# A decoder layer on one core: keys in three slots, and a third PSUM bank for the logits

## The chip, the cores and the metric

The kernel runs on one core of a Trainium2 chip, in one launch. The metric is the device time of the launch in microseconds (us). Lower is better.

## The reference

One decoder layer on x of 16 sequences, 128 positions, 256 features, in float32. Three sublayers follow each other, each with a residual and a layer norm (post-norm). The change touches the second; cut to what matters:

```python
x = _layernorm(x + mixer(x))             # quantized linear layers, gated scan over the features
x = _layernorm(x + xattn(x, ctx, pos))
x = _layernorm(x + ffn(x))               # quantized, 256 -> 1024 -> 256

def xattn(x, ctx, pos):                  # 32 heads of 8 features, 128 queries, 128 keys
    q = rope((x @ Wq).reshape(b, n, 32, 8), pos)
    k, v = split(ctx @ Wkv)
    k = rope(k.reshape(b, n, 32, 8), pos)
    w = softmax(einsum('bqhd,bkhd->bhqk', q, k) * 8 ** -0.5)
    return einsum('bhqk,bkhd->bqhd', w, v).reshape(b, n, 256) @ Wout + bout
```

## The kernel before

A tile is one sequence (128 positions on the partitions). There are 16 tiles. The order of the instructions on each engine is written out by hand as software pipelines: a step takes one stage of each of several tiles. Each engine has its own queue and runs it strictly in the order written; semaphores are the only ties between engines. SP's queue issues the DMAs of the attention.

**The mixer's pipeline** works on 8 groups of two tiles (steps 0 to 8 alone). Then three steps (`BESIDE`, here k = 0 to 2) of the mixer stand beside the first three attention steps, with the transposes of the feed-forward weights among them. From step s = 3 the attention runs alone, to s = 21; the feed-forward layer begins beside s = 18.

**An attention step s** works on tile s-1 (logits of chunks 0 to 2), s-2 (chunk 3 and the row maxima), s-3 (transposed logits, exp, values), s-4 (heads and output). A chunk is 8 heads; a tile has 4. In the code, the number after `lag` is the distance.

- `logits` (PE, L1061): 8 float16 matmuls of 32 rows by 128 columns for a chunk. Four heads k for each of two row groups b of the array, b alternating: row group `R * (j + b)`, output bank b. `rowmax` (DVE, L969) then takes one maximum over the two banks. All chunks use the same two banks, so a chunk's matmuls wait for the maximum of the chunk before.
- `maxima`: PE transposes the tile's maxima (L1072), DVE scales them into `MT` (L978). SP's `shifts` writes them with four DMAs (L796) as an extra row into `QT` (qt in the profile), and `logitsT(2, 0)` (PE, L1086), last but one on PE in a step, waits for them to land.
- `logitsT`, `exp` (ACT, L904) and `values` (PE, L1102: 16 float32 matmuls) take the four chunks of tile s-3 in turn. `sums` (PE, L1115) follows ACT's copy of all four (L913), and DVE's `reciprocal` (L987) and `heads` follow `sums` at the start of the next step. `output` (PE, L1135) is the last projection.
- `projections`: PE projects a key (L739) and the values of tile s-2 (L1046).

**Keys.** The 16 key tiles are made by `Key`, one for each step: from mixer step 2 on, and keys 11 to 15 in attention steps 3 to 7. `project` (PE), `copy` (ACT, L752), `rotate` (POOL, four operations from L720 to L724, result in `RK`), then a step later `cast` (DVE, L768), `low` (POOL, L777) and `transpose` (SP, L785, a transposing DMA into `KT`). There is one `RK` and two buffers `KA`.

The orders of DVE, POOL and SP in an attention step, as far as they matter:

```python
# DVE: reciprocal(4) heads(4) rowmax(2, 3) normal(6) maxima(2) rowmax(1, 0) queries(0) rowmax(1, 1)
#      residual(4) key.cast rowmax(1, 2)
# POOL: means(5) queries(0) key.low deviation(5) bias(3) queries_low(0) key.rotate
# SP: shifts(3) queries(1) key.transpose
```

SP is a step ahead in its numbering: `shifts(3)` of SP's step s+1 serves `logitsT(2, 0)` of PE's step s, and it stands right behind the `key.transpose` of step s.

Of the kernel before, what the change touches and what calls it, by code (L numbers as in the profile page):

```python
# [30 lines left out]
P = 128  # L31
# [607 lines left out]
def attention_layer(nc, ctx, res, B, S, D, H, HD):  # L639
# [23 lines left out]
    RQ = sb("RQ", [P, D]); RK = sb("RK", [P, D])  # L663
# [62 lines left out]
    class Key:  # L726


        def __init__(self, t, bank, values=False):
            self.t, self.ps_k, self.values = t, psum[:, bank, 0:D], values  # L730
            self.comes = t < B
            self.last = t - 1 if t > 0 else None
# [21 lines left out]
        def rotate(self, pool):  # L754
            if not self.comes:
                return
            pool.wait_ge(K_done, self.t + 1)
            rotate(pool, KS[:], kcos, ksin, self.t, rkA, rkB, RK, rk_prod, rk_done)

        def cast(self, dve):  # L760
            t = self.last
# [6 lines left out]
            dve.tensor_copy(ka[:, :, 0:3:2], RK[:].rearrange("p (h d) -> p h d", d=HD).unsqueeze(2)  # L768
                            .broadcast_to([P, H, 2, HD])).then_inc(k1_done, 1)

        def low(self, pool):
            t = self.last
# [4 lines left out]
            nc.gpsimd.tensor_tensor(ka[:, :, HD:2 * HD], RK[:].rearrange("p (h d) -> p h d", d=HD),  # L777
                                    ka[:, :, 0:HD], ALU.subtract).then_inc(k2_done, 1)

        def transpose(self, sp):  # L780
            t = self.last
# [102 lines left out]
    def scalar(act):  # L884
        def step(ph, *ts, key=None):
# [60 lines left out]
    def vector(dve):  # L946
        def step(ph, *ts, key=None):
# [12 lines left out]
            def rowmax(lag, c):  # L960
# [8 lines left out]
                dve.tensor_reduce(M[:, j:j + 2, n:n + 4], ps_L, AX.X, ALU.max).then_inc(max_done, 1)  # L969
# [62 lines left out]
    def tensor(pe):  # L1032
        def step(ph, *ts, key=None):
            def projections(lag):

                t = ts[lag]
                if key is not None and key.comes:
                    if t is not None:
                        wait(pe, V_done, t)
                    key.project(pe)  # L1040
                if t is None:
                    return
                wait(pe, V_done, t)
                if t > 2 and (key is None or not key.comes):
                    pe.wait_ge(K_done, B)
                pe.matmul(psum[:, 5, D:2 * D], CT[:, t], WkvS[:, D:2 * D], start=True, stop=True).then_inc(kv_done, 1)  # L1046

            def logits(lag, c):
# [4 lines left out]
                if c == 0:  # L1053
                    pe.wait_ge(QT_in[t % 2], landed(t))
                    pe.wait_ge(KT_in[t % 2], landed(t))
                wait(pe, max_done, NCH * t + c)
                n, j = slots(c)
                for k in range(4):
                    for b in range(2):
                        rows = slice(R * (j + b), R * (j + b) + R)  # L1060
                        ins = pe.matmul(ps_L[:, b, k], QT[t % NB][rows, n + k], KT[rows, t, n + k], start=True, stop=True,  # L1061
                                        tile_position=(R * (j + b), 0))
                ins.then_inc(L_done, 1)

            def maxima(lag):
# [5 lines left out]
                wait(pe, MT_done, t)  # L1071
                pe.transpose(ps_m, M[:].rearrange("p j t -> p (j t)"), ident[:]).then_inc(mT_done, 1)  # L1072
# [65 lines left out]
            logits(2, 3)  # L1138
            logitsT(3, 1)
            projections(2)  # L1140
# [16 lines left out]
    def fill_values(pool, i):  # L1157
# [8 lines left out]
                exp_done=exp_done, V_done=V_done, PO_done=PO_done)  # L1166


def ffn_weights(nc, ctx, res, w_gate, w_up, w_down, D, I):
# [22 lines left out]
    ps_t = [psum16[:, 2 + b % 2, :] for b in range(NT)]  # L1192
# [262 lines left out]
def decoder_layer(nc, x, ctx_in, pos, Wi, Wf, Wg, Wo, gnw, Wq, Wkv, Wout, bout, w_gate, w_up, w_down, out):  # L1455
# [6 lines left out]
    with ExitStack() as ctx:  # L1462
# [55 lines left out]
        def attention_key(s):  # L1518

            t = M_KEYS + s - BESIDE  # L1520
            return attn["Key"](t, 5) if BESIDE <= s and t <= B else None

        with nc.Block() as block:
# [65 lines left out]
            def _(act):  # L1589
# [4 lines left out]
                for s in range(M_END + 1):  # L1594
# [7 lines left out]
                    if s >= M_END - ffw["n_w"] and s < M_END:  # L1602
                        ffw["magnitudes"](act, s - M_END + ffw["n_w"])
# [151 lines left out]
```

## Time and profile before

| | |
|---|---|
| runs | 430.48, 429.61, 425.11 us (median 429.61) |
| profiled execution | 427.01 us, span 425.3 us |
| mean granted TensorE clock | 0.828 of full speed (2.4 GHz) |
| busy | PE 69%, DVE 68%, ACT 56%, POOL 49% |
| mixer alone and start | 0 to about 107 us |
| mixer beside attention | about 107 to 160.59 us |
| attention steps 3 to 9 | 160.59 to 270.90 us |
| attention steps 10 to 16 | 270.90 to 327.36 us |
| last attention steps and feed-forward | 327.36 to 425.3 us |

Read it by stages: the span is a row of stages with different limits, and the granted clock is 1.0 in some and 0.5 in others. A step's start is the start of PE's `logits(2, 3)`.

### The profile page before, as it was taken

What the parts mean: (1) busy time and instruction counts of PE and PEld (TensorE: products, weight loads), DVE (VectorE), ACT (ScalarE), POOL (GpSimd) and SP (SyncE); (2) the same over time, 40 slices, a digit from 0 to 9 for tenths busy, and PEclk for the clock granted to TensorE, in tenths of its full rate; (3) what the DMA queues carried; (4) which work ended last, traced back from release to release, by engine and by line L of the source; (5) the groups of instructions that cost most, each with busy time, mean ns of one, the idle gap of its engine ahead of it and who ended that gap; (6) DMA issues with size and microseconds to landing.
All of it is one profiled execution on the core that took longest, in us unless ns stands there. A gap on an engine that the chain in (4) does not pass through costs nothing.

```text
span 425.3 us, 9278 instructions
## 1 busy us (share of the span) xinstructions
PE 294.7 (69%) x3172; PEld 192.9 (45%) x3172; DVE 287.3 (68%) x627; ACT 238.9 (56%) x473; POOL 208.9 (49%) x489
## 2 busy tenths in 40 slices
PE   0353677876754676649459496999999847888972
PEld 0232455654543443435336253656666523455541
DVE  3878699998757755246244442888888346999982
ACT  4263467888522214325235233777767734899994
POOL 3322478666597536360642614455541202467674
PEclk9995689999775659577586655999999868999998
DMA  7980011121111212120211202121120000011011
GB/s 212 330 218 20 2 25 25 27 40 35 25 25 26 49 29 40 35 48 6 51 27 27 50 2 52 28 53 28 30 48 9 2 0 0 3 37 37 27 36 63
DMA packets 50744, 19.43 MB, mean 46 GB/s; under 512 B 42000, under 2 KB 49936, under 8 KB 50704
## 3 DMA queue, kind: packets, MB, share of 16 engines
q1 hardware_dynamic: 50704, 18.90, 18.8%
q8 instruction: 24, 0.39, 0.4%
q14 instruction: 16, 0.13, 0.1%
HBM read 8.27 MB, written 2.10 MB: 24 GB/s over the span
## 4 chain that ended last, share of the span: by engine, by line
PE 35%; DVE 16%; issue 9%; POOL 7%; ACT 6%; SPq 5%; DMA 3%; DVEq 1%; POOLq 0%; ACTq 0%
PE psum L1102 8%; PE psum L1061 5%; PE psum L1086 5%; DVE M L969 4%; PE psum L1135 3%; SPq L796 3%; DMA qt<-MT 3%; PE psum L1046 3%; PE psum L1403 2%; SPq L785 2%; PE psum L1115 2%; PE psum L379 2%; ACT region_k L1203 1%; PE psum L739 1%; DVE region_q L1378 1%
## 5 line engine op out<-in xcount | busy, mean ns | idle before, releaser
L904 ACT ACTIVATE region_a<-psum,exp_scale 128x1024 f32<-128x1024 f32 x64 | 71.3, 1115 | 67.9 <-PE psum L1086 67.8
L969 DVE TENSOR_REDUCE M<-psum 128x8 f32<-128x1024 f32 x64 | 78.2, 1222 | 22.5 <-PE psum L1061 22.2
L1086 PE MATMUL psum<-qt,KT 32*128 32x128 f16 x512 | 30.0, 246 | 36.9 <-DMA qt<-MT 35.2
L1102 PE MATMUL psum<-region_a,region_k 128*32 128x128 f32 x1024 | 46.4, 305 | 0.3 <-ACT region_a L904 0.3
L777 POOL TENSOR_TENSOR KA<-RK,KA 128x256 f16<-128x256 f32 x16 | 10.8, 676 | 60.9 <-DVE KA L768 60.8
L1086 PEld LDWEIGHTS psum<-qt,KT 32*128 32x128 f16 x512 | 18.3, 106 | 47.2 <-DMA qt<-MT 36.8
L1403 PE MATMUL psum<-FW,FXT 128*128 128x512 f16 x128 | 31.0, 386 | 7.3 <-DVE FXT L1383 5.4
L1061 PE MATMUL psum<-KT,qt 32*128 32x128 f16 x512 | 28.7, 238 | 9.7 <-DVE M L969 8.0
L1102 PEld LDWEIGHTS psum<-region_a,region_k 128*32 128x32 f32 x1024 | 26.7, 118 | 17.4 <-issue 13.4
L987 DVE RECIPROCAL rs<-psum 128x32 f32<-128x32 f32 x16 | 5.6, 353 | 37.3 <-PE psum L1115 37.3
L1061 PEld LDWEIGHTS psum<-KT,qt 32*128 32x128 f16 x512 | 16.3, 101 | 24.6 <-DVE M L969 13.6
L913 ACT ACTIVATE region_a<-psum 128x512 f32<-128x512 f32 x16 | 9.6, 597 | 25.6 <-PE psum L1102 25.6
L1346 ACT ACTIVATE region_q<-psum,gs 128x512 f32<-128x512 f32 x32 | 20.5, 680 | 5.9 <-PE psum L1403 5.9
L1403 PEld LDWEIGHTS psum<-FW,FXT 128*128 128x128 f16 x128 | 11.5, 99 | 23.2 <-issue 6.5
L1378 DVE TENSOR_TENSOR region_q<-region_q,psum 128x512 f32<-128x512 f32 x32 | 20.8, 683 | 1.7 <-ACT region_q L1346 1.4
L379 PE MATMUL psum<-WqS,X1T 128*128 128x256 f32 x64 | 21.3, 491 | 0.3 <-DVE wmean L1212 0.3
L1135 PE MATMUL psum<-WoutS,region_a 128*128 128x256 f32 x64 | 20.9, 455 | 0.5 <-ACT region_a L922 0.5
L1387 DVE TENSOR_REDUCE habs<-region_q 128x1024 f32 (+1 forms) x16 | 19.5, 1217 | 0.4 <-issue 0.3
L1360 ACT ACTIVATE region_q<-region_q,hq 128x1024 f16<-128x1024 f32 x16 | 18.4, 1148 | 1.5 <-POOL hq L1327 1.2
L869 POOL TENSOR_TENSOR t<-y2var,eps 128x1 f32<-128x1 f32 x16 | 3.1, 191 | 29.9 <-ACT junk L931 29.9
L978 DVE TENSOR_SCALAR MT<-psum 32x128 f16<-32x128 f32 x16 | 4.5, 279 | 19.0 <-PE psum L1072 19.0
L1421 PE MATMUL psum<-FW,region_g 128*128 128x256 f16 x128 | 16.6, 272 | 0.7 <-DVE X L1391 0.7
(209 smaller groups left out, 805.9 us busy)
## 6 DMA issues: line engine op xcount, KB each, us to landing
X<-in_x_dram SPq DMA_DIRECT2D x4, 512.0 KB, 6.9
out_dram<-X SPq DMA_DIRECT2D x16, 128.0 KB, 1.7
region_k<-in_L_ffn_w_gate_dram SPq DMA_DIRECT2D x1, 1024.0 KB, 11.4
region_k<-in_L_ffn_w_up_dram SPq DMA_DIRECT2D x1, 1024.0 KB, 9.8
region_k<-in_L_ffn_w_down_dram SPq DMA_DIRECT2D x1, 1024.0 KB, 10.8
qt<-MT SPq DMA_DIRECT2D x64, 2.0 KB
region_w<-in_L_attn_Wi_dram SPq DMA_DIRECT2D x1, 256.0 KB, 3.6
region_w<-in_L_attn_Wf_dram SPq DMA_DIRECT2D x1, 256.0 KB, 3.5
```

Source lines behind the costliest of these rows:

```text
L379: ins = pe.matmul(ps_y[:, k], X1T[:, k, j], WqS[:, j], start=(j == 0), stop=(j == DC - 1))
L904: act.activation(PB[c % 2], ps_P, ACT.Exp, scale=exp_scale[:, 0:1]).then_inc(exp_done, 1)
L969: dve.tensor_reduce(M[:, j:j + 2, n:n + 4], ps_L, AX.X, ALU.max).then_inc(max_done, 1)
L1061: ins = pe.matmul(ps_L[:, b, k], QT[t % NB][rows, n + k], KT[rows, t, n + k], start=True, stop=True, tile_position=(R * (j + b), 0))
L1086: ins = pe.matmul(ps_P[:, b, k], KT[rows, t, n + k], QT[t % NB][rows, n + k], start=True, stop=True, tile_position=(R * (j + b), 0))
L1102: ins = pe.matmul(ps_v[R * g:R * g + R, c], V[t % NV][:, h], PB[c % 2][:, g // 2, 2 * (g % 2) + e], start=(e == 0), stop=(e == 1), tile_po ...
L1135: ins = pe.matmul(ps_y, ATT[:, n], WoutS[:, n], start=(n == 0), stop=(n == DC - 1))
L1346: act.activation(SG[:, half(n)], ps_gate[n], ACT.Silu, scale=gs[:, n, col(t1_)]).then_inc(sg_done[n], 1)
L1360: act.activation(UH[:], HH[:, ph], ACT.Copy, bias=ROUND, scale=hq[:, col(t2)]).then_inc(uh_done, 1)
L1378: dve.tensor_tensor(hh[:, half(n)], SG[:, half(n)], ps_up[n], ALU.mult).then_inc(hh_done[n], 1)
L1387: dve.tensor_reduce(habs[:, col(t1_)], hh, AX.X, ALU.max, apply_absolute_value=True).then_inc(habs_done, 1)
L1403: ins = pe.matmul(psx[n], XT[:, c], w[c][:, half(n)], start=(c == 0), stop=(c == DC - 1))
```

## The change

- The logits get a third PSUM bank. Chunks alternate between banks 0-1 and 1-2. A chunk's eight matmuls are cut in two calls of four. A call has one row group and one bank: the first goes to the bank that the chunk before doesn't use (or that was read already), the second to the bank that the two share, after the maximum. The banks of the transposed logits, of the maxima and of the weight transposes move up by one; the maxima now share a bank with the projections, so `projections` waits for `MT` and moves behind `maxima` and `values(3, 1)`.
- `RK` becomes two buffers, and a key's way takes a step more: `cast` is done for key t-1, but `low` and `transpose` for key t-2. DVE's `cast` moves ahead of `rowmax(1, 1)`.
- ACT copies the key after `exp(3, 3)`, and `heads(4)` moves ahead of it. The three `magnitudes` of the feed-forward weights (L1203) move from mixer steps 5 to 7 to steps 2 and 3 (one, two). Some waits on banks move with them.

```diff
-    RQ = sb("RQ", [P, D]); RK = sb("RK", [P, D])
+    RQ = sb("RQ", [P, D]); RK = [sb(f"RK{i}", [P, D]) for i in range(2)]
...
-    ps_L = psum[:, 0:2, :].rearrange("p b (h k) -> p b h k", k=P)
-    ps_P = psum[:, 2:4, :].rearrange("p b (h k) -> p b h k", k=P)
-    ps_m = psum[0:H, 4, 0:P]
+    ps_L = [psum[:, n:n + 2, :].rearrange("p b (h k) -> p b h k", k=P) for n in range(2)]
+    ps_P = psum[:, 3:5, :].rearrange("p b (h k) -> p b h k", k=P)
+    ps_m = psum[0:H, 5, 0:P]
...
-            self.last = t - 1 if t > 0 else None
+            self.turned = t - 1 if 0 <= t - 1 < B else None
+            self.split = t - 2 if 0 <= t - 2 < B else None
...
         def cast(self, dve):
-            t = self.last
+            t = self.turned
...
         def low(self, pool):
-            t = self.last
+            t = self.split
...
         def transpose(self, sp):
-            t = self.last
+            t = self.split
...
             exp(3, 2)
+            heads(4)
+            exp(3, 3)
             if key is not None:
                 key.copy(act)
             values(2)
-            heads(4)
-            exp(3, 3)
             sums(3)
...
             rowmax(1, 0)
             queries(0)
+            if key is not None:
+                key.cast(dve)
             rowmax(1, 1)
             residual(4)
-            if key is not None:
-                key.cast(dve)
             rowmax(1, 2)
...
             def projections(lag):
                 t = ts[lag]
-                if key is not None and key.comes:
-                    if t is not None:
-                        wait(pe, V_done, t)
+                if t is None:
+                    return
+                pe.wait_ge(MT_done, t + 1)
+                if key is not None:
                     key.project(pe)
...
-            def logits(lag, c):
+            def logits(lag, c, second):
...
-                wait(pe, max_done, NCH * t + c)
+                wait(pe, max_done, NCH * t + c - 1 + second)
                 n, j = slots(c)
+                b = c % 2 if not second else 1 - c % 2
+                rows = slice(R * (j + b), R * (j + b) + R)
                 for k in range(4):
-                    for b in range(2):
-                        rows = slice(R * (j + b), R * (j + b) + R)
-                        ins = pe.matmul(ps_L[:, b, k], QT[t % NB][rows, n + k], KT[rows, t, n + k], start=True, stop=True,
-                                        tile_position=(R * (j + b), 0))
-                ins.then_inc(L_done, 1)
+                    ins = pe.matmul(ps_L[c % 2][:, b, k], QT[t % NB][rows, n + k], KT[rows, t, n + k], start=True,
+                                    stop=True, tile_position=(R * (j + b), 0))
+                if second:
+                    ins.then_inc(L_done, 1)
...
-            logits(2, 3)
+            logits(2, 3, 1)
             logitsT(3, 1)
-            projections(2)
             values(3, 0)
             logitsT(3, 2)
             maxima(2)
             heads(4)
-            logits(1, 0)
+            logits(1, 0, 0)
+            logits(1, 0, 1)
+            logits(1, 1, 0)
             values(3, 1)
+            projections(2)
             logitsT(3, 3)
+            logits(1, 1, 1)
+            logits(1, 2, 0)
             values(3, 2)
-            logits(1, 1)
             output(4)
+            logits(1, 2, 1)
+            logits(1, 3, 0)
             values(3, 3)
-            logits(1, 2)
             logitsT(2, 0)
             sums(3)
...
-                    if s >= M_END - ffw["n_w"] and s < M_END:
-                        ffw["magnitudes"](act, s - M_END + ffw["n_w"])
+                    if s == 2:
+                        ffw["magnitudes"](act, 0)
+                    if s == 3:
+                        ffw["magnitudes"](act, 1)
+                        ffw["magnitudes"](act, 2)
```

## Rows read from the trace of the kernel before

**Rows 1.** Windows by attention step: us, busy us by engine (instructions), granted clock, DMA share

```profile
160.59:175.09 14.50, 7.69 (x139) 4.97 (x141) 5.85 (x7) 5.50 (x8) 10.99 (x19) 0.81 0.20 40
225.79:242.65 16.86, 11.04 (x146) 7.09 (x147) 7.20 (x12) 6.36 (x11) 7.29 (x15) 0.70 0.17 33
242.65:261.01 18.36, 13.27 (x144) 8.02 (x145) 7.29 (x12) 6.09 (x10) 5.20 (x11) 0.50 0.16 30
261.01:270.90 9.89, 9.45 (x146) 6.00 (x147) 7.01 (x12) 6.13 (x10) 3.73 (x8) 0.79 0.15 29
295.05:303.13 8.08, 7.63 (x143) 4.96 (x143) 6.77 (x12) 6.03 (x10) 4.54 (x10) 1.00 0.19 36
```

**Rows 2.** Chain that ended last, step 7: start us, us, what

```profile
235.94 1.23 SPq L785
237.22 0.64 SPq L796
...
239.26 1.69 DMA qt<-MT
241.00 0.61 PE psum L1086 x8
```

**Rows 3.** Timeline of step 7: start us, us, engine, line, [idle before <-releaser]

```profile
230.68 0.28 DVE L978 TENSOR_SCALAR MT<-psum 32x128 f16<-32x128 f32 x1 [2.58 <-PE psum L1072]
231.37 0.38 ACT L752 ACTIVATE KS<-psum 128x256 f32<-128x256 f32 x1
234.75 0.42 DVE L768 CAST KA<-RK 128x512 f16<-128x512 f32 x1
235.25 0.67 POOL L777 TENSOR_TENSOR KA<-RK,KA 128x256 f16<-128x256 f32 x1 [9.34 <-DVE KA L768]
237.97 0.62 POOL L720 TENSOR_TENSOR rkA<-KS,kcos 128x256 f32<-128x256 f32 x1
239.60 0.72 POOL L724 TENSOR_TENSOR RK<-rkA,rkB 128x256 f32<-128x256 f32 x1
```

**Rows 4.** Timeline of step 13, no key in it

```profile
294.11 0.66 PE L1115 MATMUL psum<-ident,region_a 128*128 128x128 f32 x4 [0.17 <-ACT region_a L913]
295.05 0.40 PE L1061 MATMUL psum<-KT,qt 32*128 32x128 f16 x8 [0.28 <-DVE M L969]
295.28 0.39 PE L1086 MATMUL psum<-qt,KT 32*128 32x128 f16 x8
295.60 0.70 PE L1046 MATMUL psum<-WkvS,region_t 128*128 128x256 f32 x2
295.63 1.22 DVE L969 TENSOR_REDUCE M<-psum 128x8 f32<-128x1024 f32 x1
296.23 0.64 PE L1102 MATMUL psum<-region_a,region_k 128*32 128x128 f32 x16
297.20 0.28 PE L1072 MATMUL psum<-ident,M 128*32 128x128 f32 x1
300.83 0.64 PE L1102 MATMUL psum<-region_a,region_k 128*32 128x128 f32 x16
```

**Rows 5.** Page, costliest groups: shapes xcount | busy, mean ns | idle before

```profile
L904 ACT ACTIVATE region_a<-psum,exp_scale 128x1024 f32<-128x1024 f32 x64 | 71.3, 1115 | 67.9 <-PE psum L1086 67.8
```

**Rows 6.** Timeline, k = 2: transposes of the weights, over the whole array

```profile
146.69 1.07 PE L1238 MATMUL psum<-ident,region_w 128*128 128x128 f16 x16 [0.43 <-DVE region_w L1222]
```

**Rows 7.** Timeline, DVE's scan in mixer step 4, and ACT in step 3

```profile
66.68 1.35 DVE L337 TENSOR_TENSOR_SCAN region_a<-region_a,psum 128x128 f32<-128x128 f32 x4
54.76 0.51 ACT L230 ACTIVATE junk<-region_g,rg 128x256 f16<-128x256 f32 x1 [1.81 <-DVE region_g L301]
```

**Rows 8.** Chain that ended last, mixer steps 5 and 6

```profile
75.20 1.36 DVE region_a L337 x4
...
84.88 1.36 DVE region_a L337 x4
...
87.38 1.89 ACT region_k L1203 x2
```

More of the change, by code:

```diff
@@ L757, in rotate @@
             pool.wait_ge(K_done, self.t + 1)
-            rotate(pool, KS[:], kcos, ksin, self.t, rkA, rkB, RK, rk_prod, rk_done)
+            rotate(pool, KS[:], kcos, ksin, self.t, rkA, rkB, RK[self.t % 2], rk_prod, rk_done)
         def cast(self, dve):
-            t = self.last
+            t = self.turned
             if t is None:
@@ L1036, in projections @@
                 t = ts[lag]
-                if key is not None and key.comes:
-                    if t is not None:
-                        wait(pe, V_done, t)
-                    key.project(pe)
                 if t is None:
                     return
-                wait(pe, V_done, t)
-                if t > 2 and (key is None or not key.comes):
-                    pe.wait_ge(K_done, B)
+                pe.wait_ge(MT_done, t + 1)
+                if key is not None:
+                    key.project(pe)
                 pe.matmul(psum[:, 5, D:2 * D], CT[:, t], WkvS[:, D:2 * D], start=True, stop=True).then_inc(kv_done, 1)
-            def logits(lag, c):
+            def logits(lag, c, second):
                 t = ts[lag]
@@ L1052, in logits @@
                     return
[L1053 removed]
+                if c == 0 and not second:
                     pe.wait_ge(QT_in[t % 2], landed(t))
                     pe.wait_ge(KT_in[t % 2], landed(t))
[L1056 removed]
+                wait(pe, max_done, NCH * t + c - 1 + second)
                 n, j = slots(c)
+                b = c % 2 if not second else 1 - c % 2
+                rows = slice(R * (j + b), R * (j + b) + R)
                 for k in range(4):
[L1059 to L1063 removed]
+                    ins = pe.matmul(ps_L[c % 2][:, b, k], QT[t % NB][rows, n + k], KT[rows, t, n + k], start=True,
+                                    stop=True, tile_position=(R * (j + b), 0))
+                if second:
+                    ins.then_inc(L_done, 1)
             def maxima(lag):
@@ L1071, in maxima @@
                 wait(pe, MT_done, t)
+                wait(pe, V_done, t)
+                if key is not None:
+                    pe.wait_ge(K_done, min(key.t, B))
+                elif t > 2:
+                    pe.wait_ge(K_done, B)
                 pe.transpose(ps_m, M[:].rearrange("p j t -> p (j t)"), ident[:]).then_inc(mT_done, 1)
@@ L1191, in ffn_weights @@
     WT2_done = sem("fWT2_done")
-    ps_t = [psum16[:, 2 + b % 2, :] for b in range(NT)]
+    ps_t = [psum16[:, 3 + b % 2, :] for b in range(NT)]
     ps_tot = psum[:, 1, 0:n_w]
@@ L1520, in attention_key @@
             t = M_KEYS + s - BESIDE
-            return attn["Key"](t, 5) if BESIDE <= s and t <= B else None
+            return attn["Key"](t, 5) if BESIDE <= s and t < B + 2 else None
         with nc.Block() as block:
@@ L1691, in _ @@
                     mixer["steps"].at(mix, M_END + 1 + k, key=mixer_key(M_END + 1 + k))
+                    pe.wait_ge(banks["f"], NG)
+                    pe.wait_ge(banks["h"], NG)
                     ffw["transposes"](pe, k)
@@ L1697, in _ @@
                     if k == 2:
-                        pe.wait_ge(banks["h"], NG)
                         pe.wait_ge(banks["ni"], NG)
@@ L1705, in _ @@
                 pe.wait_ge(banks["x1T"], NG)
+                pe.wait_ge(attn["K_done"], M_KEYS)
                 pe.wait_ge(banks["y"], NG)
```

11 lines of the change are left out of this document (6 added, 5 removed).

## The prediction

> **What bounds the kernel now.** I read the windows by attention step first [rows 1]. A step with a key in it takes 14.5 (step 3), 16.9 (step 7; steps 4 to 6 are within 0.4 us of it) or 18.4 us (step 8, where the key is only cast and turned). A step with none takes 8.08. Steps 3 to 8 are 100.4 us for six tiles. The work isn't twice as much: PE is busy for 11.0 of 16.9 us, and it ran at a granted clock of 0.70 on the mean, against 7.6 of 8.08 at 1.0.
>
> Then the chain that ended last in such a step [rows 2]: it leaves the compute engines. SP's key transpose at 235.94, four shift DMAs from 237.22, their landing, and PE only goes on with `logitsT(2, 0)` at 241.00. The timeline says why [rows 3]: `MT` was ready at 230.96, but SP began the shifts 6.3 us later, because the key's transpose stands before them in its queue and waits for `low` on POOL, which waited 9.34 us for DVE's `cast`, which stands near the end of DVE's order. Nothing in that chain needs the key in this step. And PE, idle 5.8 us each time, comes back at half clock: 0.50 over all of step 8.
>
> In a step without a key [rows 4] the cycle is another. From the start of `sums` (294.11) over DVE's reciprocal, heads and `rowmax(2, 3)` (ends 296.85) to `maxima` (297.20, some 0.21 later than it could), from there 3.63 us of PE's order to `values(3, 3)` (300.83), then 1.36 to the next `sums` (294.11 + 8.08 = 302.19) over ACT's copy. PE has under 0.5 us idle in it.
>
> **Part 1: the key's way (RK in two slots, low and transpose a step later, cast earlier).** The cast of the key was made a step before, so `low` has nothing to wait for but POOL's own order: after the key's copy on ACT come rotate (237.97 to 240.32, 2.35 us [rows 3]), means 0.2, the query's rotate (the same four operations, 2.35) and low 0.67, so about 5.6 us from copy to `low`. Where the copy ends in the new order, from the step's start: `maxima` at 2.2 (as now), heads, three halves and `values(3, 1)` to 3.9, two projections to 5.1, `logitsT(3, 3)`, `exp(3, 3)` 0.43 later for 1.11 us [rows 5], copy 0.38 [rows 3]: 7.1. So `low` ends at 12.7, or 2.7 into the next step of 10 us. SP's transpose takes 1.28 (235.94 to 237.22), to 4.0; `MT` comes at 2.8; shifts take 3.78 from SP's start to the landing (237.22 to 241.00 [rows 2]) and land at 7.8. PE asks for them at about 8.6. So the idle 5.8 us goes, with 0.8 us to spare, and what is late next is PE's own order. A floor follows: 10.6 us from copy to landing and 8.1 from there over the step's end to the copy after make 18.7 for two steps, 9.35 each. POOL's work in a key step is 7.7 us and doesn't bind. The earlier cast (0.42) lies in DVE's idle before `rowmax(1, 1)`; without that cover it would cost 0.4.
>
> **Part 2: the logits in halves.** Eight matmuls of a chunk start within 0.23 us (295.05 to 295.28 [rows 4]): they alternate between two row groups, and pairs run together, a pair each 56 ns. A half has one row group, so its four have no partner. Each must stream its 128 columns alone: the nearest row is the 16 transposes of 128 columns over the whole array, 1.07 us or under 67 ns each, about 57 without the end of the last [rows 6]. So a half costs 0.22, as much as a chunk before, and PE pays about 0.9 us more a step. Two halves one after the other have different groups and overlap by one matmul (0.05).
> It doesn't buy what it is for: after a maximum, DVE waits for four matmuls in place of eight, and both take 0.23, and at half clock 0.6 until the last is through (the eight at 241.00 [rows 2]). So the round of maximum and logits stays.
> The Trainium skill ("TensorE: Matmul & The Clock Gate", The mechanism) says that weight loads overlap running matmuls only where the row group differs. By it a half would be dearer still (rival 3). Rows speak against it: pairs come every 56 ns in two groups, so each load lay beside a matmul of its own group.
>
> **Part 3: projections behind maxima.** Before, they filled PE's wait for `rowmax(2, 3)`, at no cost; now they stand on the cycle: 0.63 each (295.60 to 296.23 [rows 4]), twice in a key step.
>
> **The step after.** Without a key: 8.08, less the 0.21 of slack, plus 0.63, plus the halves between `maxima` and `values(3, 3)`: seven of 0.22 for two chunks of 0.22, less four overlaps of 0.05, so 0.92. Sum 9.42, 1.34 slower than now. Bounds: 8.84 if a half costs half a chunk; 9.9 with no overlap and 0.1 for each of two more switches between float16 and float32 work. With a key: 9.42 and 0.6, 10.0 at full clock; bounds 9.4 and 10.8.
>
> **The stages.** Upstream: in k = 1 and 2, at half clock, a chunk's first maximum waits for eight matmuls in a row, about 0.43 more, and (1, 3, 0) adds 0.43: 1.8 us for both (0 to 2.5). ACT's magnitudes: scan to scan is 8.52 us in mixer steps without (66.68 to 75.20 [rows 7, 8]) and 9.68 with one, 9.91 and 9.67 in the two others, so taking three of 1.89 [rows 8] out gives 3.7. Put behind step 2, the first lies in ACT's idle of 1.81 [rows 7]. The pair behind step 3 delays ACT by 3.4 to 3.8 where about 1.1 is slack: 2.7 lost. Net 1.0 gained, between 3.7 gained and 2 lost. Step 3 starts 0.8 later, at 161.4.
> Step 3: POOL still comes from the mixer with rotate of key 10 (160.73 + 0.8), the query's rotate, low, then SP 1.28 and shifts 3.78: landing at 172.0, and 0.9 of PE to the step's end, so 11.5 us in place of 14.5. Steps 4 to 7: four of 10.0 for 67.6. Steps 8 to 16: nine of 9.42, 84.8, in place of 18.4 + 9.9 + 56.5. Step 17 starts at 161.4 + 11.5 + 40.1 + 84.8 = 297.8, before at 327.4: 29.6 us earlier. The tail hangs on `MT` (offset 2.5 in place of 2.3): +0.2. The feed-forward layer and the waits on banks that moved find their work long done: 0, else some tenths.
> So 427.01 - 29.4 = 397.6 us for the profiled execution, about 398. That execution lies 2.6 under the median of the runs, 429.61, and inside their range; a median after may lie up to 2 higher.
>
> **Rivals.**
> 1. *The key path still binds in part.* POOL's chain has 0.8 us to spare; if ACT's copy or a POOL operation is later, each us beyond it comes back in four steps, and short idles then could bring half clock back in some. 2 us late in each and one step of 13: 403 to 412. For it: POOL's queue is the fullest in step 3. Against: all its durations are rows.
> 2. *Halves are cheap* (matmuls of one group overlap as pairs do): 13 steps 0.6 faster, about 389. Only a lack of rows speaks for it.
> 3. *A half pays its weight loads*, 0.44 in place of 0.22: seven more of 0.22 in each of 13 steps, 20 us, so 418. The pace of pairs [rows 4] speaks against it.
> 4. *The change doesn't do what it says, and it is slower.* SP's shifts stay behind a key not ready, since `low` stands behind POOL's rotate of the query. Steps 3 to 8 keep their 100.4 us, and steps 9 to 16 lose 1.34 each, with 1.8 upstream and nothing gained: near 440. It decides where less than about 2.4 us of the 6.9 in each key step comes back.
> 5. *Half clock.* Step 8 took 18.4 with 5.1 idle, so 13.3 of work at 0.50 [rows 1]; with the halves 15.7. Each attention step at half clock costs some 6 us, and from the fifth on the kernel is slower: 430 to 480. Against: steps 10 to 16 stayed at 1.0 with pauses under 0.5; the new order has two pauses, of 0.75 and 0.46. The Trainium skill (same page, A second HAM failure mode: psum-queue depth-cycling) tells of a kernel whose cycling over PSUM banks paused PE briefly and made the clock swing; no row here shows that.
>
> **How the numbers follow.** The forecast 0.68, rival 1 0.12, rival 2 0.08, rival 3 0.05, rivals 4 and 5 together 0.07. The ends 386 (cheap halves and the whole of the magnitudes' gain) and 412 (key path late in part, upper bounds) hold the first three, 0.88 less what bounds of several terms at once may exceed. A measurement of this kernel tells about 2% (8.6 us) from no change: faster by over 2% is all up to about 420, so 0.90 with most of rival 3; 0.04 within; 0.06 slower.
>
> **What would show it.** In the profile after: PE's L1086 no longer waits for qt<-MT by 5.8 us, and POOL's L777 no longer 9 us for DVE L768; windows of steps 4 to 7 near 10 at clock 1.0; steps 10 to 16 near 9.4, with PE's transposes of M waiting for DVE again and four matmuls of L1061 spaced 56 ns; scans 8.5 apart in mixer steps 5 to 8. Steps without a key at 8.1 or less would refute parts 2 and 3; key steps over 12 us part 1.

## The result

| | before | after |
|---|---|---|
| median of the runs | 430.05 us (425.11 to 431.16) | 416.24 us (414.52 to 436.38) |
| profiled execution | 427.01, span 425.3 | 415.0, span 413.2 |
| mean granted clock | 0.828 | 0.811 |

The ratio is 0.969, 95% interval 0.958 to 0.979. The change makes the kernel faster: by 14 us in the medians, and by 12.0 us in the profiled executions, where 29.4 were forecast (427.01 to 397.6). A run whose clock lay under that of the other runs of its kernel (here the one of 436.38 us, clock 0.749) counts in the medians and ranges, but not in the ratios, here and in the table further down.

The stages first. Windows of the kernel after by step (us, then busy us of PE, PEld, DVE, ACT and POOL with their instructions, granted clock, DMA share, GB/s), to set against [rows 1]: step 3; steps 4 to 7; steps 8 to 16; then a step at full clock and one at half.

```profile
157.36:169.09 11.73, 10.24 (x138) 6.52 (x138) 6.55 (x7) 5.42 (x7) 9.60 (x16) 0.65 0.33 38
169.09:214.38 45.29, 40.71 (x573) 25.97 (x572) 28.27 (x46) 24.43 (x39) 30.33 (x58) 0.79 0.32 52
214.38:315.69 101.31, 94.12 (x1270) 58.30 (x1270) 62.05 (x99) 54.26 (x82) 37.68 (x75) 0.71 0.17 28
223.21:232.05 8.84, 7.85 (x143) 5.01 (x142) 6.87 (x11) 5.98 (x10) 5.17 (x11) 1.00 0.38 58
263.41:277.05 13.64, 13.26 (x142) 8.13 (x142) 6.95 (x11) 6.01 (x10) 4.52 (x10) 0.50 0.13 22
```

Read the last two against each other. It is the same work. At 1.0 the step takes 8.84 us and PE has 1.0 us of pauses (8.84 less 7.85); at 0.50 it takes 13.64 and PE's own instructions fill it. Of steps 11 to 16, which stood at 1.0 throughout before, only parts stood at 1.0 after.

The waits of PE (us in total, times, longest), first the one line of the kernel before, then two of the kernel after. L1086 before and L1089 after are the transposed logits. Before, PE waited for ACT at that place in none of steps 10 to 16.

```profile
PE psum L1086 <- DMA qt<-MT: 35.2, 7, 6.2
...
PE psum L1089 <- ACT region_a L905: 8.5, 19, 0.6
...
PE psum L1089 <- DMA qt<-MT: 1.5, 2, 1.1
```

What took its place on PE is in the timeline of the step at full clock, to set against [rows 4]:

```profile
222.62 0.66 PE L1118 MATMUL psum<-ident,region_a 128*128 128x128 f32 x4 [0.39 <-ACT region_a L914]
223.21 0.39 PE L1058 MATMUL psum<-KT,qt 32*128 32x128 f16 x4
223.63 0.40 PE L1089 MATMUL psum<-qt,KT 32*128 32x128 f16 x8
223.96 0.64 PE L1105 MATMUL psum<-region_a,region_k 128*32 128x128 f32 x16
225.24 0.40 PE L1089 MATMUL psum<-qt,KT 32*128 32x128 f16 x8 [0.64 <-ACT region_a L905]
225.57 0.28 PE L1075 MATMUL psum<-ident,M 128*32 128x128 f32 x1
...
226.00 0.42 PE L1058 MATMUL psum<-KT,qt 32*128 32x128 f16 x12
226.35 0.64 PE L1105 MATMUL psum<-region_a,region_k 128*32 128x128 f32 x16
226.93 0.70 PE L1043 MATMUL psum<-WkvS,region_t 128*128 128x256 f32 x2
227.56 0.40 PE L1089 MATMUL psum<-qt,KT 32*128 32x128 f16 x8
227.79 0.40 PE L1058 MATMUL psum<-KT,qt 32*128 32x128 f16 x8
```

Two things are to be seen. `logitsT(3, 2)` at 225.24 waits 0.64 us for ACT's exp to free a bank: the values' projection, which filled that time before, now stands at 226.93. And twelve matmuls of the logits, three calls of four, start within 0.21 us (226.00 to 226.21). The values follow 0.35 us after the first of the twelve; before, what stood behind eight followed after 0.23.

The queues in a key step (step 6), to set against [rows 2, 3]:

```profile
193.01 0.72 POOL L778 TENSOR_TENSOR KA<-RK,KA 128x256 f16<-128x256 f32 x1
193.49 0.28 DVE L979 TENSOR_SCALAR MT<-psum 32x128 f16<-32x128 f32 x1 [0.28 <-PE psum L1075]
193.76 1.23 SPq L786 DMA_TRANSPOSE KT<-KA  x1
195.04 3.68 SPq L797 DMA_DIRECT2D qt<-MT  x4
...
199.82 0.40 PE L1089 MATMUL psum<-qt,KT 32*128 32x128 f16 x8 [1.05 <-DMA qt<-MT]
200.15 0.66 PE L1118 MATMUL psum<-ident,region_a 128*128 128x128 f32 x4
```

`low` waits for nobody any more; it starts as soon as POOL is through with the query. The shifts start 1.3 us after `MT`, not 6.3, and PE's wait is 1.05 us in this step; the only other one is 0.48, in step 3.

### The profile page after: what moved, and what is told of

Same layout as the page of the kernel before. It is cut to its first block, busy times and chain, and to the rows that moved or that the text cites. A ratio compares the mean times of both kernels' runs of the same rounds, so it can differ in the third digit from the quotient of the medians.

```text
span 413.2 us, 9287 instructions
## 1 busy us (share of the span) xinstructions
PE 308.6 (75%) x3172; PEld 200.0 (48%) x3172; DVE 288.3 (70%) x627; ACT 238.4 (58%) x473; POOL 209.5 (51%) x489
## 4 chain that ended last, share of the span: by engine, by line
PE 39%; ACT 9%; DVE 8%; issue 8%; POOL 8%; SPq 2%; DMA 1%; DVEq 1%; POOLq 0%; ACTq 0%
PE psum L1105 8%; PE psum L1058 5%; PE psum L1138 5%; PE psum L1089 5%; ACT region_a L905 4%; PE psum L1043 3%; PE psum L379 3%; PE psum L1118 3%; PE psum L1410 2%; ACT region_a L914 2%; SPq L797 2%; PE psum L1128 1%; DVE region_q L1385 1%; PE psum L740 1%; DMA qt<-MT 1%
## 5 line engine op out<-in xcount | busy, mean ns | idle before, releaser
L1105 PE MATMUL psum<-region_a,region_k 128*32 128x128 f32 x1024 | 52.7, 337 | 0.0
L1089 PE MATMUL psum<-qt,KT 32*128 32x128 f16 x512 | 32.8, 252 | 10.3 <-ACT region_a L905 8.5
L1058 PE MATMUL psum<-KT,qt 32*128 32x128 f16 x512 | 32.6, 261 | 6.6 <-DVE M L970 4.7
L1105 PEld LDWEIGHTS psum<-region_a,region_k 128*32 128x32 f32 x1024 | 29.8, 129 | 10.6 <-issue 4.7
L1089 PEld LDWEIGHTS psum<-qt,KT 32*128 32x128 f16 x512 | 19.2, 106 | 29.9 <-ACT region_a L905 16.2
L1058 PEld LDWEIGHTS psum<-KT,qt 32*128 32x128 f16 x512 | 19.8, 110 | 22.3 <-issue 13.3
L861 POOL TENSOR_TENSOR means<-y2sum,pair 128x2 f32<-128x2 f32 x16 | 3.2, 202 | 42.2 <-DVE X L1007 42.2
L1138 PE MATMUL psum<-WoutS,region_a 128*128 128x256 f32 x64 | 23.8, 506 | 0.5 <-ACT region_a L923 0.5
L1007 DVE SCALAR_TENSOR_TENSOR X<-psum,X 128x256 f32<-128x256 f32 x16 | 6.8, 425 | 24.2 <-PE psum L1138 24.2
L720 POOL TENSOR_TENSOR rkA<-KS,kcos 128x256 f32<-128x256 f32 x16 | 10.8, 673 | 21.7 <-ACT KS L753 21.7
L845 POOL TENSOR_TENSOR region_qa<-RQ,region_qa 128x256 f16<-128x256 f32 x16 | 11.4, 716 | 20.4 <-DVE region_qa L957 20.4
```

The source lines that it names most:

```text
L1058: ins = pe.matmul(ps_L[c % 2][:, b, k], QT[t % NB][rows, n + k], KT[rows, t, n + k], start=True, stop=True, tile_position=(R * (j + b), 0))
L1089: ins = pe.matmul(ps_P[:, b, k], KT[rows, t, n + k], QT[t % NB][rows, n + k], start=True, stop=True, tile_position=(R * (j + b), 0))
L1105: ins = pe.matmul(ps_v[R * g:R * g + R, c], V[t % NV][:, h], PB[c % 2][:, g // 2, 2 * (g % 2) + e], start=(e == 0), stop=(e == 1), tile_po ...
L1138: ins = pe.matmul(ps_y, ATT[:, n], WoutS[:, n], start=(n == 0), stop=(n == DC - 1))
```

## The experiments

Theory: the key part gives the gain, and the pause that the moved projections leave on PE brings half clock, which takes back a good part of it. Rivals: the third bank's calls or the writing ahead bring the half clock; or the projections and halves cost it by their length. Each ratio is against runs of the kernel before on the same chip (their medians are 428.1 to 430.4). The chip differs between groups of experiments, so differences of one or two us between two rows say nothing.

| kernel | median us (range) | ratio, 95% interval |
|---|---|---|
| e1 keys only | 390.74 (387.57 to 393.41) | 0.907 (0.898 to 0.917) |
| e2 all but the keys | 452.22 (447.03 to 453.66) | 1.052 (1.047 to 1.058) |
| e3 keys, projections late | 397.61 (396.58 to 399.47) | 0.926 (0.921 to 0.930) |
| e4 after, spare projection before the maxima | 408.94 (404.01 to 413.41) | none given |
| e5 keys, loops swapped | 387.90 (385.57 to 388.05) | 0.904 (0.900 to 0.908) |
| e6 after, nothing written ahead | 412.20 (402.36 to 436.69) | none given |
| e7 keys, magnitudes early | 387.24 (385.05 to 389.71) | 0.905 (0.901 to 0.909) |
| e8 the same, low first | 378.26 (376.91 to 386.55) | 0.883 (0.880 to 0.887) |
| e9 after, values' projection early | 397.81 (393.77 to 399.78) | 0.926 (0.917 to 0.936) |
| e10 the same, low first | 385.95 (380.23 to 387.95) | 0.906 (0.899 to 0.914) |
| e11 keys, thin projection | 395.64 (388.74 to 397.41) | none given |
| e12 after, the pause filled | 394.43 (391.14 to 395.14) | 0.920 (0.916 to 0.925) |
| e13 after, the pause filled in part | 400.49 (393.58 to 411.18) | 0.924 (0.917 to 0.930) |
| e14 e10 with the logits behind the values | 379.01 (377.58 to 381.70) | 0.886 (0.882 to 0.891) |

### The two parts apart: e1 and e2

e1 is before with the key part alone (RK in two slots, `low` and `transpose` a step later, `cast` ahead of `rowmax(1, 1)`); e2 is after with that taken back.

> The kernel before with the key's part of the change alone: two RK, low and transpose a step later, cast before rowmax(1, 1). Logits, banks, projections, ACT's order and the magnitudes stay. Theory A (the key's part gives some 35 us, the new order of the logits and projections costs 0.75 us a step and brings PE to half clock from step 10 on): key steps near 8.7 to 9.5 us, the others 8.08 at clock 1.0, time 387 to 393. Rival B (half clock comes with the removed stalls or from step to step, whatever the order of the logits): steps 10 to 16 fall to half clock here too, at 12 to 13 us, time 405 to 418.

> The changed kernel with the key's part taken back: one RK, cast, low and transpose one after the other as before, cast after residual(4). The third bank, the halves, the late projections and the moved magnitudes stay. Theory A: key steps 17 to 18 us as before, the others 8.8 at full clock or up to 13.6 at half clock, so slower than the kernel before by 5 (all at full clock) to 35 us (most at half). Rival B: half clock needs the key's part, the steps from 10 on stay at 1.0 and 8.83 us, time 430 to 436.

The parts have opposite signs: 40 us gained by one, 22 lost by the other. They don't quite add up (18, where the whole change gave 14). In e2 the old wait is back, 34.1 us in 6 waits for qt<-MT. In e1 the steps without a key are as before, all at full clock (windows of a key step and of eight without):

```profile
182.25:191.96 9.71, 8.09 (x144) 5.34 (x144) 7.56 (x12) 6.14 (x10) 8.73 (x17) 1.00 0.40 57
225.18:289.81 64.63, 61.07 (x1128) 39.63 (x1129) 53.76 (x88) 48.31 (x73) 33.29 (x67) 1.00 0.21 36
```

The timeline of its key step shows what is left: the shifts wait for the key's transpose, that for `low`, and `low` for POOL's rotation of the query.

```profile
185.31 0.67 POOL L778 TENSOR_TENSOR KA<-RK,KA 128x256 f16<-128x256 f32 x1
...
186.01 1.23 SPq L786 DMA_TRANSPOSE KT<-KA  x1
186.02 0.28 DVE L979 TENSOR_SCALAR MT<-psum 32x128 f16<-32x128 f32 x1 [1.04 <-PE psum L1073]
...
187.29 3.07 SPq L797 DMA_DIRECT2D qt<-MT  x4
...
191.63 0.40 PE L1087 MATMUL psum<-qt,KT 32*128 32x128 f16 x8 [1.34 <-DMA qt<-MT]
```

### Is it the order of the projections: e3 and e4

e3 is e1 with this move on PE (and ACT's copies moved as in the change); e4 is after with a spare projection in front of the maxima, its result used by nobody, and the wait for the row maxima moved behind it:

```diff
 e3           logitsT(3, 1)
-            projections(2)
...
             values(3, 1)
+            projections(2)
 e4
+                for _ in range(FILL):
+                    pe.matmul(psum[:, 5, D:2 * D], CT[:, t], WkvS[:, D:2 * D], start=True, stop=True)
+                pe.wait_ge(max_done, NCH * t + NCH)
```

> The kernel of keys alone, with the projections moved behind maxima and values(3, 1) as in the change, and ACT's copies behind exp(3, 3) and heads(4); logits whole and in two banks. It tells which of the two, halves or late projections, brings the longer step and the half clock. If it is the pause of PE before maxima that the projections left: steps near 8.5 at full clock (8.08 less 0.21 plus 0.63) and half clock in many, time 400 to 415. If it is the halves: steps 8.5 at clock 1.0, time 391 to 398.

> The changed kernel with one more projection of the values (two float32 matmuls of 256 columns, same operands, written again by the real one later) in PE's wait before maxima; it adds no output. If the clock falls because PE pauses there, it stays at 1.0 here and steps are 8.8 to 9.0: time 390 to 398, faster by 20 us than the changed kernel for more work. If the clock falls for another reason, steps from 10 on stay at 13 to 14 us: time 414 to 420.

e3's steps take 8.71 us: 0.63 more, one projection. From step 9 to 16 its clock stood at 1.0 but for three short falls, of 3.4 to 6.8 us, so it lost 7 us against e1 and not 22. By its time it lies in the range that was written down for the halves (391 to 398), not in that for the pause (400 to 415): with the same pause, the half clock of the changed kernel came here only for moments. The pause is there, too (window of six steps; timeline):

```profile
234.35:286.61 52.26, 45.76 (x846) 29.75 (x847) 40.57 (x67) 36.18 (x55) 26.81 (x54) 1.00 0.18 33
254.53 0.40 PE L1087 MATMUL psum<-qt,KT 32*128 32x128 f16 x8 [0.64 <-ACT region_a L905]
```

e4 makes each step longer (9.36 us) and the kernel faster, 409 against 416: more work on PE, less time at half clock. It hit neither of its two ranges (390 to 398, 414 to 420), and the reason is in the timeline: its filler stood behind `logitsT(3, 2)`, not in the pause, and the pause of 0.64 was still there.

### Halves: e5

```diff
-                for k in range(4):
-                    for b in range(2):
+                for b in range(2):
+                    for k in range(4):
```

> The keys-only kernel with the two loops of the logits swapped: all four matmuls of one row group, then all four of the other, in the same two banks; nothing else changes. If the prediction's cost of a half was right (four matmuls of one group stream one after the other, 0.22 us, and two halves overlap by one), a chunk takes 0.45 in place of 0.22 us, two to three such chunks lie on the cycle of 8.08 us, and the 14 steps are 0.4 to 0.7 us longer each: 396 to 401 us. If matmuls of different row groups run side by side whatever the order in which they are written, the eight start within 0.25 us as before, steps without a key stay at 8.07 to 8.10, and the time is that of keys only, 390.7 (387.5 to 393.5).

The order in which the two row groups are written costs 0.05 us a step (8.13 against 8.08) and nothing in the total. The single records show why: the eight matmuls of a chunk start in pairs (249.975 and .988, 250.041 and .054, 250.097 and .110, 250.153 and .165), as they do where the code alternates. The records don't name the row group; that each pair has one of each is read from the spacing.

```profile
249.97 0.40 PE L1062 MATMUL psum<-KT,qt 32*128 32x128 f16 x8 [0.30 <-DVE M L970]
250.21 0.39 PE L1087 MATMUL psum<-qt,KT 32*128 32x128 f16 x8
```

### What brings half clock: e6, e9, e11, e12, e13

e6 puts both calls of each chunk behind the maximum. e9 puts the values' projection back behind `logitsT(3, 1)`; ACT's copy of the values moves up, and the maxima wait for it, since they share a bank. e11 is e1 with 8 of 256 columns in that projection in steps without a key; it leaves out most of those tiles' values, so its output isn't the layer's. e12 and e13 leave the changed kernel's work where it is and add a spare matmul in the pause itself, with the waits that its bank needs.

```diff
 e9
             logitsT(3, 1)
+            project_values(2)
             values(3, 0)
 e11
-  pe.matmul(psum[:, 5, D:2 * D], CT[:, t], WkvS[:, D:2 * D], ...)
+  n = D if key is not None else 8
+  pe.matmul(psum[:, 5, D:D + n], CT[:, t], WkvS[:, D:D + n], ...)
 e12, e13 (FILL = 256, 64)
+                pe.matmul(psum[:, 5, D:D + FILL], CT[:, t], WkvS[:, D:D + FILL], start=True, stop=True)
...
             values(3, 0)
+            fill(2)
             logitsT(3, 2)
```

> The changed kernel with its banks and its calls of four, but both calls of a chunk next to each other behind the maximum, so that nothing is written ahead of a maximum; projections stay behind maxima. Theory 1: writing ahead thins PE's work between two maxima, and that is what brings half clock in steps 10 to 16. Then the clock stays at 1.0 in most of these steps, they take 8.7 to 8.8 us, and the time is 396 to 400 us, like the keys with late projections (397.6). Theory 2: the half clock comes from another part of the change (the late projections with the magnitudes' new place, or the calls of one row group). Then steps of 13 us at 0.5 come as in the changed kernel, and the time stays at 412 to 418.

> The changed kernel, third bank and writing ahead kept, with the values' projection back in PE's wait for the maxima (behind logitsT(3, 1)); so that the maxima may share its bank, ACT copies the values right behind exp(3, 1) and the maxima wait for that copy (0.38 us; by the rows of after it ends at about the time at which the maxima start now). The key's projection stays late. Theory (late projections are both the longer step and the thinner PE that brought half clock): steps without a key take 8.83 - 0.63 = 8.2 us, PE is busy for 95% of them, the clock stays at 1.0 from step 10 to 16, and the time is 388 to 392 us. Rival (the third bank, its calls of four or the magnitudes bring the half clock): steps of 8.2 at 1.0 at first, then steps of some 13 us at 0.5, and 404 to 414 us. A second rival: the copy delays exp(3, 2) and the maxima by some 0.4 us, and steps take 8.6.

> Keys only (two banks, early projections), but in steps without a key the values' projection computes 8 of its 256 columns, so PE has some 0.6 us less work in its wait for the maxima; no other operation, order or wait changes, and the values of those tiles are for the greater part left out. Theory: what brought half clock in the changed kernel is PE's work per time (7.85 busy of 8.83 us), not the third bank. Here PE is busy for about 7.0 of 8.08 us: the granted clock falls to 0.5 in several of steps 8 to 16, such steps take 12 to 13.5 us, and the time is 400 to 430 us though PE has less to do. Rival: the clock looks at something else in the change (the calls of one group, the pause before the sums), so steps stay at 8.08 and 1.0, and the time is that of keys only, 390.7 or less.

> The changed kernel with one spare projection of 256 columns (its result is used by nobody) in PE's wait of 0.64 us before logitsT(3, 2). Theory: that pause is what brings half clock in steps 10 to 16. Then they stay at 1.0 and take 8.8 to 8.9 us, although nothing of the changed kernel's own work has moved, and the time is 394 to 399 us. Rival (the pause before the sums, the third bank's calls or chance brings it): steps of 13.6 at 0.5 come as before, 410 to 418 us.

> The same with 64 columns in place of 256: the pause becomes about 0.45 us in place of 0.64. If the length of the longest pause decides, and 0.39 us didn't bring half clock in e9, this lies near that and most steps stay at 1.0: 394 to 402 us. If the whole pause has to be filled, or PE's share of busy time decides, the half clock stays: 408 to 418 us.

e12 answers it: one useless projection a step, in PE's wait, and 22 us come back, 394.4 against 416.2. The length of a step at full clock hasn't changed, 8.83 us; the time at half clock has gone. In the profiled executions steps 8 to 16 took 79.9 us (213.27 to 293.12) where the changed kernel's took 101.3. A window of six of its steps, and the place in the timeline where the pause was:

```profile
239.55:292.53 52.98, 50.44 (x859) 31.80 (x859) 40.87 (x65) 35.89 (x55) 23.57 (x48) 1.00 0.15 29
240.88 0.64 PE L1106 MATMUL psum<-region_a,region_k 128*32 128x128 f32 x16
241.46 0.70 PE L1152 MATMUL psum<-WkvS,region_t 128*128 128x256 f32 x2
242.16 0.40 PE L1090 MATMUL psum<-qt,KT 32*128 32x128 f16 x8
```

e13 has the same waits, but its filler leaves a pause of 0.27 us there. Its clock had four short falls, of 3.4 us each, from step 14 on. Its runs reach from 393.6, which is e12's time, to 411.2, so the median of 400.5 alone says little.

e6 had nothing written ahead and fell all the same, for 30.7 us in a stretch (288.2 to 318.9) like the changed kernel (253.4 to 284.1 and 290.9 to 321.6). Its runs spread over 34 us, so its median says little; that the half clock comes without the writing ahead stands on its trace. There PE waits 0.64 at the same place in each step; the five steps before the fall had that pause, too, and stood at 1.0. Its fastest run, 402.4, is 12 us under the fastest of the changed kernel, so whether the writing ahead adds to the loss is open.

e9 has the third bank, calls of four and writing ahead, and stood at 1.0 for all of seven steps; PE waits elsewhere, 0.39 before `sums` and 0.37 for `rowmax(1, 0)` (window and timeline). It missed its forecast of 388 to 392 all the same: its steps took 8.81 us, not 8.2 (e14 tells why), and its clock stood at half from 203.0 to 223.4, in steps 7 and 8.

```profile
236.52:298.21 61.69, 56.14 (x988) 35.08 (x988) 47.73 (x76) 41.07 (x64) 28.00 (x57) 1.00 0.19 31
259.29 0.41 PE L1068 MATMUL psum<-KT,qt 32*128 32x128 f16 x8 [0.37 <-DVE M L970]
```

e11 has two banks, the old order, and PE has less to do in an unchanged step. It has a pause before `logitsT(3, 2)`, of 0.32 us. Three short falls came in steps 10 to 16, where e1 had none; steps 9 to 16 took 72.4 us in its profiled execution and 64.6 in e1's. The medians, 395.6 and 390.7, point the same way, but the ranges overlap. Both windows are steps of the same work:

```profile
248.57:256.65 8.08, 7.31 (x141) 4.95 (x142) 6.77 (x12) 6.02 (x10) 4.54 (x10) 1.00 0.20 38
256.65:267.68 11.03, 10.26 (x142) 6.56 (x142) 6.87 (x12) 6.02 (x10) 4.80 (x11) 0.69 0.22 43
```

So steps can lose time by doing less: 7.8 us over eight of them here. My theory for e11 (several long falls, 400 to 430 us) was too strong, and the rival (no half clock, 390.7 or less) was wrong, too.

### The rest of the way: e7, e8, e10, e14

e7 adds the magnitudes' move to e1; e8 swaps two calls on POOL; e10 is e9 with the same swap; e14 puts the logits of e10 back behind the values.

```diff
 e8, e10       means(5)
-            queries(0)
             if key is not None:
                 key.low(pool)
+            queries(0)
 e14
-            logits(1, 1, 1)
-            logits(1, 2, 0)
             values(3, 2)
+            logits(1, 1, 1)
+            logits(1, 2, 0)
             output(4)
-            logits(1, 2, 1)
-            logits(1, 3, 0)
             values(3, 3)
+            logits(1, 2, 1)
+            logits(1, 3, 0)
```

> Keys only, and the three magnitudes moved on ACT from mixer steps 5 to 7 to steps 2 and 3, as in the change. By the prediction's term, and by the scans of the changed kernel (the sixth starts 1.08 us earlier), 1.0 us is gained: 389.7 us. If the whole of the earlier start of step 3 in the changed kernel (157.36 against 160.59 us) comes from them, 3 us: 387.5. If ACT's delay in step 3 isn't caught up, 0 to 2 lost: 391 to 393.

> As the one before, and on POOL the key's low stands ahead of the query's rotation in place of behind it (nothing it needs comes later than the step before). In keys only PE still waits 1.0 to 1.4 us for the shifts in each key step, SP's key transpose waiting for low. If that queue is the bound, low comes some 2.35 us earlier, that wait goes and the four or five key steps take 8.7 to 9.0 in place of 9.7 to 10.1: 3 to 5 us less than the one before, 385 to 387. If PE's own order or the maxima come next at once (or the query's rotation, 0.67 us later, then is late), under 1 us is gained, and the time is that of the one before.

> As the one before, and low ahead of the query's rotation on POOL, as in the kernel of 378.3 us (keys, magnitudes and low, two banks). If the third bank is worth nothing of itself once the values' projection is early, the time is that kernel's plus some 0.1 us a step: 379 to 382. If writing ahead of the maximum gains, steps under 8.0 and under 377. If the half clock comes back with it, 390 or more.

> The kernel with values' projection early, low first and the third bank (385.95), with the logits of chunks (1, 1) and (1, 2) put back behind values(3, 2) and values(3, 3), still in halves and one half ahead. There PE waits 0.37 us for rowmax(1, 0) in front of values(3, 2), and 0.33 us of logits stand in front of values(3, 3). Theory: these two and the third call (0.12) are the 0.73 between 8.81 and 8.08; steps without a key become 8.1 to 8.2, and the time is 377 to 380 us, that of two banks (378.3) within its spread. Rival 1: writing ahead then really gains on the maxima, steps under 8.0, 375 or less. Rival 2: the third bank's calls cost by themselves, steps stay at 8.5 to 8.8, 383 to 388.

e8 is the fastest kernel here (e14 is within 1 us of it), 378.3 us, 12% under before and 38 us under the change. `low` (187.05) now ends before `MT` comes (190.55), so SP's key transpose is through when the shifts may start, and PE has no wait for them. Its key step and eight steps without, windows and timeline:

```profile
186.66:195.22 8.56, 8.11 (x148) 5.34 (x144) 6.77 (x13) 6.31 (x11) 7.26 (x15) 1.00 0.35 68
211.72:276.34 64.62, 61.00 (x1128) 39.64 (x1128) 53.78 (x88) 48.17 (x73) 33.62 (x68) 1.00 0.22 39
187.05 0.67 POOL L778 TENSOR_TENSOR KA<-RK,KA 128x256 f16<-128x256 f32 x1
...
187.75 1.24 SPq L786 DMA_TRANSPOSE KT<-KA  x1
...
190.55 0.28 DVE L979 TENSOR_SCALAR MT<-psum 32x128 f16<-32x128 f32 x1 [0.93 <-PE psum L1073]
190.85 2.70 SPq L797 DMA_DIRECT2D qt<-MT  x4
...
194.66 0.39 PE L1087 MATMUL psum<-qt,KT 32*128 32x128 f16 x8
```

It gained more than expected (9 us for 3 to 5). A part of it is the clock: in e7 it fell at 210.9 for 10.2 us, and the two steps around that took 10.34 and 12.32 us; in e8 no fall came between 177.7 and 286.9, and they took 8.43 and 8.07. Another part is step 3: there `low` came at 157.70 where it came at 161.88 in e7, and the step took 9.7 us for 13.2. Of the total, 1.9 us stood already at the start of step 3, where the swap hasn't acted yet. e7's own gain over e1 can't be told from 1 us by the ratios, 0.905 and 0.907. In the traces the four scans of mixer steps 5 to 8 follow that of step 4 within 33.86 us, where e1 needs 37.71, and the scan of step 4 comes 1.2 us later.

e10 fell short of its forecast, because its steps are 8.81 us and not 8.2, though the projection is off the path. e14 shows what they are made of. With the logits behind the values its steps take 8.18 (57.27 over seven), and it reaches e8's time:

```profile
225.71:282.98 57.27, 54.11 (x987) 34.96 (x988) 47.03 (x77) 41.28 (x64) 28.36 (x58) 1.00 0.21 34
```

So the order of the calls cost 0.63 a step: PE waited for `rowmax(1, 0)` in front of `values(3, 2)`, and 0.33 of logits stood in front of `values(3, 3)`. In the changed kernel the late projections (0.63) lay in just that wait. Either one alone costs 0.6 to 0.7; both together cost 0.75. What e14 keeps of the third bank costs 0.10 a step (8.18 against 8.08) and gains nothing (379.0 against 378.3 us).

## Why the prediction was wrong

**The direction and the key part were right.** PE no longer waits for SP; the key steps at full clock took 9.26 and 9.93 us, where 9.4 to 10.8 stood; step 3 took 11.73 where 11.5 stood. The spare time of 0.8 us was slightly too hopeful: PE waited 0.48 and 1.05 us for the shifts, in steps 3 and 6. e1 puts this part at 40 us. The next bound was not PE's own order, as part 1 had it, but POOL's, as rival 1 feared: e8 removes it with one swap.

**The step that failed** is in rival 5: "Against: steps 10 to 16 stayed at 1.0 with pauses under 0.5; the new order has two pauses, of 0.75 and 0.46." The pauses were foreseen and came (0.64 and 0.39), and nothing was charged for them. They took back what the change gave: steps 8 to 16 took 101.3 us where nine at 8.83 would be 79.5, so 21.8 us; e12, which fills one of them, ran these steps in 79.9. The forecast had 84.8 for them. I had weighed half clock as a state of all attention steps, at 430 to 480 us, and held it unlikely. It came in part: 4.8 us (13.64 less 8.84) in each step that stood at 0.5, some 4.5 such steps in all. A term between nothing and all was missing from the sum and from the range. What the runs don't show is why the same pause cost so much more here than in e3.

**The halves were mis-sized**: 0.92 forecast, and 8.84 measured for the step, the lower bound. Rival 2 was right in that, and its reason, that matmuls of one group overlap as pairs do, was right only across calls: different groups run side by side even where four of one are written first (e5, and the twelve at 226.00). That gave 5.3 us over nine steps (84.8 less 79.5); here a mistake in the sum hid a part of the loss by the clock. And the price of part 3 and part 2 was added where they cover each other (e3, e10, e14).

**Upstream** was mis-sized: step 3 began at 157.36, not at 161.4. DVE's scan that starts mixer step 8 came 1.08 us earlier (103.38 for 104.46), as forecast (1.0), and both terms of that were right: from the scan of step 4 to that one it is 33.88 us for 37.78, so 3.9 gained where 3.7 stood, and the scan of step 4 comes 2.8 later (69.50 for 66.68) where 2.7 stood. From that last scan to step 3 it is 53.98 us for 56.13. The 1.8 us charged to k = 1 and 2 for halves in a row didn't come, and some 2.2 us more I can't place.

The stages, each against its forecast: step 3 began 4.0 us early, then step 3 took 0.2 too long, steps 4 to 7 took 5.2 (two of them partly at half clock) and steps 8 to 16 took 16.5 (21.8 for the clock less 5.3 for the halves). That is 17.9 at the start of step 17, and 17.4 in the time. It was luck that it wasn't more: without the early start and the cheap halves, neither of them in the sum, it would have been some 26.7.

**Rival 1** holds in kind (POOL's order) but was worth about 1 us in a key step, and didn't decide; **rival 3** is refuted by e5. **Rival 4** is refuted in size: the shifts still stand behind the key's transpose, but start 1.3 us after `MT` in place of 6.3, and key steps at full clock took some 7 us less.

## What to carry to other kernels

Work on TensorE that "costs nothing" because it lies in a wait may be what holds the clock. Before moving it, write down what the pause left behind would cost if the granted clock fell in every step behind it, and put that into the sum as a case of its own; a spare matmul put in the pause itself tests it. Costs of two moves on the same cycle don't add: see first which wait each would lie in. And when a step that waited is taken off a queue, look at what stands in front of the next one: here the kernel with two calls on POOL swapped was 9 us faster, though some of that was the clock's.

## What the runs showed of the hardware

- **Matmuls of different row groups run side by side, and not in the order written.** In the changed kernel at half clock, four matmuls of the logits and eight of the transposed logits, written one call after the other, start mixed (the third and fourth of L1058 start behind the first of L1089, which is written after them):

```profile
264.46 0.39 PE L1058 MATMUL psum<-KT,qt 32*128 32x128 f16 x2
264.55 0.28 PE L1089 MATMUL psum<-qt,KT 32*128 32x128 f16 x1
264.65 0.31 PE L1058 MATMUL psum<-KT,qt 32*128 32x128 f16 x1
264.65 0.28 PE L1089 MATMUL psum<-qt,KT 32*128 32x128 f16 x1
264.75 0.31 PE L1058 MATMUL psum<-KT,qt 32*128 32x128 f16 x1
```

The Trainium skill ("TensorE: Matmul & The Clock Gate", The mechanism) says that matmuls start and end in program order, without reordering. The starts in this trace don't agree, and the pairs in e5 point the same way; nor does the sentence in the section on the kernel before, that each engine runs its queue strictly in the order written, hold for these starts. Of the ends, which are modelled, no run here can tell.

- **The clock.** In steps 10 to 16 it fell from 1.0 to 0.5 in the seven profiled executions in which PE waited before `logitsT(3, 2)` in each step, for 0.27 to 0.64 us: the changed kernel, e2, e3, e4, e6, e11, e13. In the nine without a pause at that place it stayed at 1.0 in these steps: before, e1, e5, e7 to e10, e12, e14. The pause doesn't bring a fall each time: in e2 and e6 five of these steps passed at 1.0 with a pause of 0.64 in each. PE's share of busy time doesn't separate them: e13 fell with 0.92, e9 stayed up with 0.91. That filling the pause holds the clock is shown (e12); what it is in the pause that decides, its place, its length or something that goes with it, is open. So is why a fall in these steps lasted 3.4 to 10.2 us in e3, e4, e11 and e13, and up to 30.7 in the changed kernel, e2 and e6. In the changed kernel and e6 PE was busy for over 97% of a fall of 30.7 us (29.94 and 29.92 of 30.70 us). The Trainium skill (same page, A second HAM failure mode: psum-queue depth-cycling) puts swings of the clock down to cycling over PSUM banks with short pauses. The pauses agree with this trace; the banks don't: e9, e10, e12 and e14 cycle over the same three and stayed at 1.0 in these steps, and e3 and e11 fell with two.
